# First-rank slots cut from 44 to 22, with a listed tail per graph

## The chip, the cores and the metric

One core of one Trainium2 chip runs the whole program. The metric is device time in microseconds (us) of one execution. A profiled execution has a span, from its first to its last instruction, and a little time around it.

## What is computed

The input is eight graphs of 1,024 nodes with 128 features, and for each graph a 1,024 x 1,024 0/1 adjacency matrix. The layer first takes, for each node, the maximum over the (normalised) features of its first 25 neighbours, and then applies a small mixture-of-experts network to each tile of 128 nodes. Cut to what matters:

```python
scores = jnp.where(A != 0, -arange(N), -inf)
vals, idx = top_k(scores, 25)                 # the 25 lowest-numbered neighbours
agg = where(valid, X[idx], -inf).max(axis=2)  # X = layernorm(x)
agg = where(degree <= 25, maximum(agg, 0), agg)
x = x + relu(concat([X, agg]) @ W + b)        # gnn
h = relu(layernorm(x) @ Wi.T + bi)            # ffn, 2 expert layers, one expert per tile of 128
for l in range(2): h = relu(h @ (mean Ws[l] + Wr[l, e]).T + biases + h)
out = x + h @ Wo.T + bo
```

The chance of an edge falls with the node numbers of both its ends, so the first 128 nodes (the hub tile) have many neighbours, and the other 896 have few: in the inputs used, at most 23.

## The kernel before

The program works on one graph per stage. `positions()` walks ten stages (s = 0 to 9) of NS = 44 positions each. Every engine walks the same list, and its work for position p of stage s is written by tables (`MASK_AT`, `RANK_AT`, `TOP_AT`, `GATHER_AT`, `LAYER_AT` and so on). The order on each engine is thus fixed; engines meet only through semaphores. In stage s three graphs are in work: graph s is prepared (`prepare`), the slots of graph s-1 run (`slot`, `one_hot`, `fold_slot`), and the network of graph s-2 runs (`finish`).

Preparing a graph: ScalarE (ACT) turns adjacency rows into a bf16 mask (line 714), SyncE (SP) issues a DMA that transposes it into `at` (L421), and TensorE (PE) multiplies each 128-row tile of `at` by a triangular matrix (L869). The result `rank[j, i]` says that node j is the r-th neighbour of node i within j's tile of 128 (a value from 201 on says that it is none). ACT copies it out (L641).

A slot serves one pair (tile group g, rank r). A one-hot matrix `onehot = (rank == r)` is made by GpSimd (POOL, L547), by VectorE (DVE, L975), or by ACT in one or two steps (L670 and L687, or L681 for r = 1). PE multiplies the features of the tile by it, once for each of the two parts into which the float32 features are split (L777), which puts the feature row of the r-th neighbour under each node. DVE folds the slot into one of two running maxima (L988). There are two slot banks in PSUM, so PE waits for the fold of the slot before last. A one-hot is 896 columns wide, or less where `CAPS` says that no further tile of nodes needs that rank. One group holds two tiles, 5 and 6. `CAPS` has up to 10 ranks for the first tile and 4 to 6 for the others: 44 pairs.

The hub tile goes another way: DVE finds the 25 neighbours with rounds of max and match-replace (L1039 to L1061), POOL fetches one row per neighbour with 25 indirect DMAs (L535), and DVE reduces them (`reduce_half`). In stage 1 the expert weights are also folded and stored (L908, L1153).

`merge` (L995) joins both maxima after the last slot. `check_totals` (L1177) tests at the end whether any node exceeded its caps; if so, `again` recomputes its tile alone. In the profiled execution no such tile is recomputed.

## Time and profile before

| what | us |
|---|---|
| median of 3 runs | 738.79 (737.64 to 739.55) |
| span of the profiled execution | 734.5 |
| PE busy | 611.5 (83%) |
| DVE busy | 574.2 (78%) |
| POOL busy | 541.9 (74%) |
| ACT busy | 521.2 (71%) |
| DMA, mean rate | 179 GB/s |

The profiled execution's own time is its span of 734.5 us and about 4.3 us around it. Busy time is a union: a pipelined matmul overlaps the next, so the busy time of a group of matmuls contains part of its neighbours' time. The granted clock of PE is given as a share of 2.4 GHz: 0.50 means 1.2 GHz.

### The profile page before, as it was taken

The page shows a single profiled execution, that of the slowest core. Times are in us where ns is not written, and L with a number is a line of the kernel's source. Part 1 is how long each engine was busy: PE and PEld are TensorE (multiplying, and loading weights), DVE is VectorE, ACT ScalarE, POOL GpSimd, SP SyncE. Part 2 cuts the span into 40 slices and gives each one's busy share as a digit, 9 for nine tenths or more (in the row PEclk, how much of TensorE's full clock was granted, in tenths as well). Part 3 has the DMA queues.
Part 4 walks back from the last instruction along what each step waited for, and adds up shares of the span by engine and source line. Part 5 has one row for each costly group of instructions (what it writes and reads, how often), then busy time and mean ns, then how long its engine had stood idle before and what let it go on. Part 6 is the DMA issues. An engine that isn't in the chain of part 4 may idle for free.

```text
span 734.5 us, 11755 instructions
## 1 busy us (share of the span) xinstructions
PE 611.5 (83%) x3496; PEld 502.9 (68%) x3497; DVE 574.2 (78%) x959; ACT 521.2 (71%) x981; POOL 541.9 (74%) x388
## 2 busy tenths in 40 slices
PE   0466666679999799979997999899987999799686
PEld 0054545566987588858885888668875988588565
DVE  3766799878987898779987898789878987777740
ACT  5672455369977898779876987699769985478062
POOL 4577488497979987898878897989799878984000
PEclk9986798898999899979998999989998999799989
DMA  9999997479746965496638755785474543045222
GB/s 298 305 196 265 314 344 241 134 176 293 226 132 158 267 175 152 102 259 205 166 109 222 236 163 142 190 240 159 127 182 124 161 138 87 22 113 144 58 72 77
DMA packets 145171, 131.73 MB, mean 179 GB/s; under 512 B 72219, under 2 KB 112324, under 8 KB 145092
## 3 DMA queue, kind: packets, MB, share of 16 engines
q1 hardware_dynamic: 128124, 105.94, 53.5%
q0 software_dynamic: 7296, 15.74, 8.3%
q10 hardware_dynamic: 9680, 9.21, 4.5%
q8 instruction: 31, 0.51, 0.3%
q14 instruction: 40, 0.33, 0.1%
HBM read 98.20 MB, written 17.98 MB: 158 GB/s over the span
## 4 chain that ended last, share of the span: by engine, by line
PE 59%; DVE 22%; issue 5%; DVEq 4%; DMA 4%; ACT 4%; SPq 1%; ACTq 0%
PE slot_ps L777 28%; PE ffn_ps L842 11%; DVE acc L988 9%; PE ffn_ps L852 4%; PE ffn_ps L826 4%; PE prep_ps L869 3%; DMA at<-mask 2%; PE ffn_ps L811 2%; PE ffn_ps L792 2%; DVEq L1060 2%; DVE top L1047 2%; PE ffn_ps L812 2%; DMA adj_sb<-in_adj_dram 2%; DVE wst L1153 1%; DVE score L1049 1%
## 5 line engine op out<-in xcount | busy, mean ns | idle before, releaser
L777 PE MATMUL slot_ps<-onehot,xsplit 128*128 128x512 f32 (+3 forms) x1376 | 375.5, 401 | 51.1 <-DVE acc L988 44.4
L988 DVE TENSOR_TENSOR acc<-slot_ps,acc 128x896 f32<-128x896 f32 (+2 forms) x336 | 293.7, 884 | 77.3 <-PE slot_ps L777 74.5
L547 POOL TENSOR_SCALAR onehot<-rank,ranks 128x896 fp32r<-128x896 bf16 (+3 forms) x128 | 298.4, 2333 | 72.6 <-PE slot_ps L777 67.5
L777 PEld LDWEIGHTS slot_ps<-onehot,xsplit 128*128 128x128 f32 x1376 | 251.9, 204 | 105.7 <-issue 71.0
L535 POOL DMA_INDIRECT gath<-feature_table,idx x200 | 207.7, 1038 | 47.9 <-issue 42.6
L842 PE MATMUL ffn_ps<-hT,wst 128*128 128x128 f32 x1024 | 135.1, 277 | 0.0
L842 PEld LDWEIGHTS ffn_ps<-hT,wst 128*128 128x128 f32 x1024 | 129.0, 191 | 5.9 <-issue 0.8
L670 ACT ACTIVATE away<-rank,ranks 128x896 bf16<-128x896 bf16 (+4 forms) x136 | 107.9, 793 | 6.8 <-DVE wst L1153 6.4
L687 ACT ACTIVATE onehot<-away 128x896 fp32r<-128x896 bf16 (+4 forms) x136 | 96.3, 708 | 21.5 <-PE slot_ps L777 10.6
L629 ACT ACTIVATE hT<-ffn_ps,wst 128x128 f32<-128x128 f32 x256 | 81.1, 375 | 29.5 <-PE ffn_ps L842 27.3
L641 ACT ACTIVATE rank<-prep_ps 128x448 bf16<-128x448 f32 x128 | 63.0, 550 | 21.0 <-PE prep_ps L869 11.7
L714 ACT ACTIVATE mask<-adj_sb 128x1024 bf16<-128x1024 uint32 x56 | 58.0, 1047 | 25.8 <-DMA at<-mask 20.9
L681 ACT ACTIVATE onehot<-rank,ranks 128x896 fp32r<-128x896 bf16 (+1 forms) x48 | 56.0, 1167 | 22.1 <-PE slot_ps L777 21.3
L869 PE MATMUL prep_ps<-at,before 128*128 128x448 bf16 x128 | 39.9, 380 | 15.0 <-DMA at<-mask 12.3
L908 PE MATMUL ffn_ps<-ident,hT 128*128 128x128 f32 x136 | 26.5, 329 | 28.8 <-DVE wst L1153 25.7
L908 PEld LDWEIGHTS ffn_ps<-ident,hT 128*128 128x128 f32 x136 | 18.8, 169 | 38.8 <-issue 36.7
L1047 DVE MAX8 top<-score 128x8 f32<-128x1024 f32 x32 | 39.0, 1219 | 0.3
L975 DVE TENSOR_SCALAR onehot<-rank,ranks 128x1792 fp32r<-128x1792 bf16 (+2 forms) x40 | 38.5, 962 | 0.7 <-PE slot_ps L777 0.7
L826 PE MATMUL ffn_ps<-xnT,wiT 128*128 128x512 f32 x64 | 33.4, 611 | 0.5 <-ACT xnT L618 0.5
L852 PE MATMUL ffn_ps<-woT,hT 128*128 128x128 f32 x256 | 32.8, 281 | 0.0
L869 PEld LDWEIGHTS prep_ps<-at,before 128*128 128x128 bf16 x128 | 11.4, 99 | 30.9 <-DMA at<-mask 12.4
L852 PEld LDWEIGHTS ffn_ps<-woT,hT 128*128 128x128 f32 x256 | 29.8, 191 | 3.6 <-issue 3.6
(121 smaller groups left out, 586.3 us busy)
## 6 DMA issues: line engine op xcount, KB each, us to landing
wst<-folded_weights SPq DMA_DIRECT2D x128, 257.0 KB, 2.9
adj_sb<-in_adj_dram SPq DMA_DIRECT2D x64, 512.0 KB, 5.9
folded_weights<-wst ACTq DMA_DIRECT2D x34, 256.0 KB, 6.9
hT<-in_L_ffn_Wr_dram SPq DMA_DIRECT2D x26, 256.0 KB, 10.3
xs<-in_x_dram SPq DMA_DIRECT2D x8, 512.0 KB, 8.1
feature_table<-xn SPq DMA_DIRECT2D x8, 512.0 KB, 4.1
x<-in_x_dram SPq DMA_DIRECT2D x8, 512.0 KB, 4.3
out_dram<-h SPq DMA_DIRECT2D x16, 256.0 KB, 2.4
```

Of the source, the lines that this page charges most:

```text
L535: pool.indirect_dma_start(gath[:, j, :], None, tables[b], bass.IndirectOffsetOnAxis(ap=idx[:, b % 2, 0, j:j + 1], axis=0)).then_inc(signal ...
L547: pool.tensor_scalar(onehot[:, UNIT[n]:UNIT[n] + many, 0:wide * P], rank[:, b % 2, first:first + many, 0:wide * P], ranks[:, r - 1:r], Non ...
L629: ins = act.activation(hT[:, 1 - l, j, i, :], ffn_ps[(i + 1) % 2][:, j * P:(j + 1) * P], ACT.Relu, bias=wst[:, i, HC * HID + j:HC * HID + ...
L641: act.activation(rank[:, s % 2, jt, c * CW:(c + 1) * CW], prep_f[c][:, 0:CW], ACT.Copy, bias=float(NONE)).then_inc(s_q, 1)
L670: act.activation(away[:, i % AWAYS, 0:wide * P], rank[:, b % 2, first, 0:wide * P], ACT.Square, bias=ranks[:, r - 1:r], scale=-1.0).then_i ...
L687: act.activation(onehot[:, UNIT[n], 0:wide * P], away[:, i % AWAYS, 0:wide * P], ACT.Relu, bias=1.0, scale=-1.0).then_inc(s_acthot, 1)
L777: mm = pe.matmul(slot_ps[n % 2][:, c0:c1], xsplit[:, b % 2, part, first + j, :], onehot[:, UNIT[n] + j, c0:c1], start=(j == 0 and part == ...
L826: pe.matmul(ffn_ps[1 - j][:, :], wiT[:, j * P:(j + 1) * P], h0T[:, 4 * g:4 * g + 4, :].rearrange("p t c -> p (t c)"), start=True, stop=Tru ...
L842: mm = pe.matmul(ffn_ps[(i + 1) % 2][:, j * P:(j + 1) * P], wst[:, i, c0:c0 + P], hT[:, l, kc, i, :], start=(kc == 0), stop=(kc == HC - 1))
L852: mm = pe.matmul(o, hT[:, 0, kc, i, :], woT[:, kc, :], start=False, stop=(i % 4 == 3 and kc == HC - 1))
L869: mm = pe.matmul(prep_f[c][:, 0:CW], before[:, :], at[:, jt, cols], start=True, stop=not second)
L988: dve.tensor_tensor(acc[:, p % 2, 0:cols], slot_ps[n % 2][:, 0:cols], acc[:, p % 2, 0:cols], ALU.max).then_inc(s_max, 1)
```

## The change

The two-dimensional `CAPS` become one number per source tile, 5, 3, 3, 3, 2, 2, 2, 2, for all 896 nodes: 22 pairs. Every slot is 896 columns wide, and no group holds two tiles. A stage now has NS = 46 positions, and a slot comes at every second one, so a stage has 23 slots: the 22 and a last one for the crowd.

The crowd of a graph is the nodes that have more neighbours in some source tile than the cap. They are listed (at most 128), and what their slots missed (at most 7 neighbours each) is fetched. The steps for graph s-1 in stage s:

- SP stores the last row of `rank` (the counts per tile) at position 37 of stage s-1, as before, and now loads it back at position 40 in pieces of 8 nodes (`counts`).
- DVE compares with the caps and scans (position 1), PE sums over the pieces (2), DVE makes a place for each crowd node (3), PE turns it into a list with 8 small matmuls (4), DVE forms row numbers and columns (5).
- POOL fetches the 128 adjacency rows, 4 KB each, with one indirect DMA (6). ACT makes a mask of them (11), SP transposes it (12), PE ranks it with 8 matmuls of 128 columns (17), DVE keeps the entries beyond the caps and takes the top 8 (18 to 20).
- POOL fetches 7 feature rows for each crowd node, one indirect DMA each (23 to 28). DVE takes their maximum (33), ACT and POOL split it (34, 35), DVE makes a one-hot with which node each list place belongs to, and PE puts them back in slot 22, at position 44.

`x` of the next graph has one buffer instead of two, and is loaded after the feature table is stored. The positions of some other steps move. `check_totals` tests the tail and the length of the list instead. Cut to its core:

```diff
+CAPS = [5, 3, 3, 3, 2, 2, 2, 2]
+TAIL = 7
 PLACES = [
-          (1, 3), (5, 1), (6, 2), (1, 2), (3, 6), (0, 4), ...   # 44
+          (0, 2), (0, 1), (1, 1), (0, 3), (1, 2), (2, 1), (2, 2), (0, 4), (1, 3), (3, 1), (2, 3), (4, 1),
+          (3, 2), (3, 3), (5, 1), (0, 5), (4, 2), (6, 1), (5, 2), (7, 1), (6, 2), (7, 2)]
-NS = len(SLOTS)
+CROWD = len(PLACES)
+NSL = len(PLACES) + 1
+NS = 2 * NSL
-ACT_HOT = [0, 1, 2, 4, 6, 8, 9, 11, 14, 17, 21, 22, 25, 26, 29, 30, 32, 34, 35, 37, 39, 40, 41]
-POOL_HOT = [3, 5, 7, 10, 12, 15, 16, 18, 23, 27, 28, 31, 33, 36, 38, 43]
+POOL_HOT = [0, 4, 8, 12, 16, 20]
+DVE_HOT = [7, 15, CROWD]
+ACT_HOT = [k for k in range(NSL) if k not in POOL_HOT and k not in DVE_HOT]
...
-               {16: 0, 18: 1, 20: 2, 22: 3, 28: 4, 32: 5, 37: 6, 38: 7}]
+               {19: 0, 21: 1, 23: 2, 25: 3, 27: 4, 29: 5, 32: 6, 35: 7}]      # RANK_AT
-              [11, 13, 17, 20, 21, 22, 25, 27]]
+              [11, 13, 15, 17, 21, 23, 25, 27]]                              # TOP_AT
-    REDUCE_AT = {14: (0, 0, 0), 24: (0, 0, 1), 31: (0, 1, 0), 34: (0, 1, 1)}
+    REDUCE_AT = {9: (0, 0, 0), 24: (0, 0, 1), 30: (0, 1, 0), 37: (0, 1, 1)}
+    TAIL_AT = {23: [0], 24: [1, 2], 25: [3], 26: [4], 27: [5], 28: [6]}
...
-        xs = sb("xs", [P, 2, IT, C])
+        xs = sb("xs", [P, IT, C])
...
+                if 1 <= s <= B and p == CROWD_MASK_AT + 1:                   # SP
+                    sp.wait_ge(s_mask, n + 1)
+                    sp.dma_start_transpose(ct[:, :, :], mask[:, n % MASKS, :]).then_inc(s_turn[n % MASKS], 16)
...
+                if s < B and p == COUNT_LOAD_AT:
+                    sp.wait_ge(s_cstore[s % 2], 16 * (s // 2 + 1))
+                    sp.dma_start(counts[0:PIECES, :, :], totals_d[s].rearrange("j (p c) -> p j c", c=EIGHT)
+                                 ).then_inc(s_count, 16)
...
+                if p == FETCH_AT:                                            # POOL
+                    pool.wait_ge(s_fetch, b + 1)
+                    pool.indirect_dma_start(crow[:, :], None, adj_rows,
+                                            bass.IndirectOffsetOnAxis(ap=fetch[:, 0:1], axis=0)
+                                            ).then_inc(s_crow, 16)
+                for i in TAIL_AT.get(p, []):
+                    if i == 0:
+                        pool.wait_ge(s_cidx, b + 1)
+                    pool.indirect_dma_start(tail[:, i, :], None, tables[b],
+                                            bass.IndirectOffsetOnAxis(ap=cidx[:, i:i + 1], axis=0)
+                                            ).then_inc(s_tail, 16)
...
+                if p == CROWD_MASK_AT:                                       # ACT
+                    act.wait_ge(s_crow, 16 * (b + 1))
+                    act.activation(mask[:, n % MASKS, :], crow[:, :].bitcast(U32), ACT.Sign).then_inc(s_mask, 1)
...
+                if p == OFFSET_AT:                                           # PE
+                    pe.wait_ge(s_upto, b + 1)
+                    pe.matmul(prep_f[0][0:PIECES, 0:EIGHT], strict[0:PIECES, 0:PIECES], upto[0:PIECES, :],
+                              start=True, stop=True).then_inc(s_offset, 1)
+                if p == LIST_AT:
+                    pe.wait_ge(s_place, b + 1)
+                    for c in range(EIGHT):
+                        mm = pe.matmul(prep_f[1][:, 0:4], hot[0:PIECES, c, :], ids[0:PIECES, c, :],
+                                       start=(c == 0), stop=(c == EIGHT - 1))
+                if p == BEYOND_AT:
+                    pe.wait_ge(s_turn[n % MASKS], 16 * (n // MASKS + 1))
+                    for jt in range(IT):
+                        mm = pe.matmul(prep_f[half][:, place_ * P:(place_ + 1) * P], ct[:, jt, :],
+                                       beyond[:, STEP_OF[jt], :], start=True, stop=True)
...
-                    second = [f for f, many in GROUPS if many == 2 and f + 1 == jt]
-                        if second:
-                            mm = pe.matmul(prep_f[c][:, 0:CW], onesb[:, :], at[:, jt - 1, cols],
-                                           start=False, stop=True)
...
+                if p == FLAG_AT:                                             # DVE
+                    dve.wait_ge(s_count, 16 * (b + 1))
+                    step(dve.scalar_tensor_tensor(out=kept[0:PIECES], in0=counts[0:PIECES], scalar=NONE - 0.5,
+                                                  in1=unkept[0:PIECES], op0=ALU.is_ge, op1=ALU.mult))
+                    step(dve.tensor_tensor(kept[0:PIECES], kept[0:PIECES], counts[0:PIECES], ALU.add))
+                    step(dve.tensor_tensor(kept[0:PIECES], kept[0:PIECES], limit[0:PIECES], ALU.is_gt))
+                    step(dve.tensor_reduce(flag[0:PIECES, :], kept[0:PIECES].rearrange("p j c -> p c j"), AX_X, ALU.max
+                                           ).then_inc(s_flag, 1))
...
+                if p == TAIL_MAX_AT:
+                    dve.wait_ge(s_tail, 16 * TAIL * (b + 1))
+                    dve.tensor_reduce(tail_max, tail.rearrange("p k c -> p c k"), AX_X, ALU.max).then_inc(s_tailmax, 1)
```

## Rows read from the trace of the kernel before

**Rows 1.** Windows: stages 1, 4, 8 (busy, clock, DMA share, GB/s); below them L995.
```profile
core 0: us, PE busy (x) PEld busy (x) DVE busy (x) ACT busy (x) POOL busy (x), PEclk, DMA share, GB/s
48.00:147.90 99.90, 67.61 (x317) 51.96 (x317) 81.83 (x129) 45.51 (x67) 67.37 (x48) 0.79 0.92 254
303.50:381.10 77.60, 71.88 (x422) 60.46 (x421) 66.09 (x106) 65.12 (x126) 66.34 (x43) 0.93 0.69 181
614.00:688.80 74.80, 68.51 (x405) 58.39 (x404) 55.01 (x84) 43.40 (x89) 50.90 (x32) 0.93 0.33 89
...
L995 DVE TENSOR_TENSOR aggT<-acc x8: 1091/1093/1093, 146.8 to 687.7; 128x896 f32<-128x896 f32 x8
```

**Rows 2.** Windows: positions 0 to 18, 19 to 34, 35 to 43 of stage 4.
```profile
302.30:338.10 35.80, 31.27 (x149) 24.31 (x148) 28.07 (x49) 29.60 (x56) 31.15 (x20) 0.86 0.85 218
338.10:366.60 28.50, 27.83 (x200) 25.95 (x198) 26.06 (x38) 25.52 (x56) 25.70 (x16) 1.00 0.56 155
366.60:380.00 13.40, 12.88 (x78) 10.30 (x76) 12.04 (x22) 10.46 (x15) 9.59 (x7) 1.00 0.53 146
```

**Rows 3.** Groups by line in stage 4: busy us, mean ns, idle before.
```profile
L777 PE MATMUL slot_ps<-onehot,xsplit 128*128 128x512 f32 (+3 forms) x172 | 47.2, 401 | 5.7 <-DVE acc L988 5.6
L547 POOL TENSOR_SCALAR onehot<-rank,ranks 128x896 fp32r<-128x896 bf16 (+3 forms) x17 | 40.2, 2366 | 5.5 <-PE slot_ps L777 5.0
L988 DVE TENSOR_TENSOR acc<-slot_ps,acc 128x896 f32<-128x896 f32 (+6 forms) x42 | 36.8, 884 | 8.6 <-PE slot_ps L777 8.2
L535 POOL DMA_INDIRECT gath<-feature_table,idx x25 | 26.1, 1044 | 5.9 <-issue 5.3 <-DVE idx L1061 0.7
L670 ACT ACTIVATE away<-rank,ranks 128x896 bf16<-128x896 bf16 (+4 forms) x18 | 13.9, 771 | 0.0
L687 ACT ACTIVATE onehot<-away 128x896 fp32r<-128x896 bf16 (+4 forms) x19 | 13.3, 701 | 0.7
L629 ACT ACTIVATE hT<-ffn_ps,wst 128x128 f32<-128x128 f32 x32 | 10.2, 378 | 3.0 <-PE ffn_ps L842 2.7
L641 ACT ACTIVATE rank<-prep_ps 128x448 bf16<-128x448 f32 x16 | 7.9, 553 | 1.1 <-PE prep_ps L872 0.6 <-PE prep_ps L869 0.4
L681 ACT ACTIVATE onehot<-rank,ranks 128x896 fp32r<-128x896 bf16 (+1 forms) x6 | 7.0, 1168 | 1.5 <-PE slot_ps L777 1.5
L1047 DVE MAX8 top<-score 128x8 f32<-128x1024 f32 x4 | 4.9, 1219 | 0.0
L975 DVE TENSOR_SCALAR onehot<-rank,ranks 128x1792 fp32r<-128x1792 bf16 (+2 forms) x5 | 4.5, 905 | 0.0
```

**Rows 4.** The same, shapes kept apart.
```profile
L547 POOL TENSOR_SCALAR onehot<-rank,ranks 128x896 fp32r<-128x896 bf16 x14 | 37.3, 2671 | 5.4 <-PE slot_ps L777 5.0
L988 DVE TENSOR_TENSOR acc<-slot_ps,acc 128x896 f32<-128x896 f32 x28 | 30.1, 1084 | 7.4 <-PE slot_ps L777 7.1
```

**Rows 5.** PE's instructions in order: start us, us, what.
```profile
347.38 1.06 PE L777 MATMUL slot_ps<-onehot,xsplit 128*128 128x512 f32 x4
348.29 1.05 PE L842 MATMUL ffn_ps<-hT,wst 128*128 128x128 f32 x8
```

**Rows 6.** Windows inside positions 5 to 11 of stage 4.
```profile
316.00:321.00 5.00, 2.25 (x6) 1.45 (x6) 4.33 (x18) 1.95 (x4) 4.31 (x5) 0.74 1.22 260
321.00:326.00 5.00, 3.54 (x12) 3.04 (x12) 3.95 (x6) 5.00 (x11) 4.65 (x4) 0.50 0.89 188
```

**Rows 7.** DVE's L1057, 25 elements a row: all eight executions, ns.
```profile
L1057 DVE TENSOR_SCALAR spread<-top,lane x8: 231/2246/2250, 34.1 to 587.7; 128x25 f32<-128x25 f32 x8
```

**Rows 8.** Time to landing of the transposes (`at`), then of adjacency tiles.
```profile
DMA to landing us min/median/max: 3.2/5.6/14.2
...
DMA to landing us min/median/max: 3.5/5.9/9.4
```

**Rows 9.** Windows: stage 1 in two parts, same columns as Rows 1.
```profile
48.00:110.00 62.00, 41.49 (x190) 31.73 (x190) 48.10 (x76) 28.17 (x43) 43.36 (x33) 0.78 1.12 298
110.00:147.90 37.90, 26.12 (x128) 20.23 (x127) 33.72 (x54) 17.34 (x24) 24.01 (x16) 0.82 0.59 182
```

481 lines of the change are left out of this document (312 added, 169 removed), and 5 rows, old and new, of the table PLACES.

## The prediction

> **What bounds the kernel now.** I read the windows by stage first. Stages 2 to 7 are alike: about 77.5 us each (the eight merges of L995 begin at 146.8 to 687.7, seven steps of 77.3 on average [rows 1]), and stage 4 stands for them. In it PE is busy 71.9 of 77.6 us, POOL 66.3, DVE 66.1, ACT 65.1, and DMA has a share of 0.69 [rows 1]. POOL also has 5.3 us of issue gaps between its gathers that count as idle [rows 3], which makes 71.6. So no engine stands alone as the bound: PE is first, POOL is level with it, and the others are 6 us behind. The stage is 1.08 times the busiest engine.
>
> Then the stage in three parts, because its limits differ [rows 2]. In positions 19 to 34 (28.5 us) PE is busy 27.8 at full clock: there PE is the bound. In 35 to 43 (13.4 us) it is so again, 12.9. In positions 0 to 18 (35.8 us) PE shows 31.3, but at a mean clock of 0.86; the norm, the transposes of `h0` and the fold of slots hand over to each other there, and for some 10 us PE runs at half clock (a mean of 0.86 is 28% of the time at 0.50): after a stretch in which it was busy 2.25 of 5 us the granted clock is 0.50, the 1.2 GHz level [rows 6]. PE's idle time before slots, 5.7 us, ends with DVE's fold [rows 3]. DMA is full around these rows, share 0.89 to 1.22 [rows 6]. The three parts add up to 77.7.
>
> **The change on each engine, stage 4.**
>
> PE. The old slots stream 71,168 columns per graph (the sum over `SLOTS` of width x tiles x 2 parts), the new ones 23 x 2 x 896 = 41,216. A slot of 1,792 columns with its four matmuls takes 348.29 - 347.38 = 0.91 us of PE [rows 5], 0.508 ns a column, so 29,952 columns fewer are 15.2 us. The second matmuls of the two-tile group go too (2 x 2 of 448 columns at the same rate, 0.5 us with the pipeline). Added are 17 small matmuls; the trace has none of 4 to 8 columns, so they lie between 0.05 and 0.15 us each (8 matmuls of 128 columns take 1.05 us from first to last [rows 5], 0.13 each, and most of these stream less): 0.9 to 2.6, I take 1.3. PE: 71.9 - 15.2 - 0.5 + 1.3 = 57.5.
>
> DVE. Folds: 36.8 for L988 [rows 3] and 2.2 for the first two (L986, priced as two full folds of 1.084 [rows 4]) become 23 x 1.084 = 24.9, 14.1 less. The one-hots, 4.5 [rows 3], become three of 896 columns, half of the 1,792 form, some 0.6 each: 2.7 less. The crowd adds: five small instructions with drains at position 1, at 0.2 to 0.3 each, 1.3; the place with its compare of 1,024 elements, priced as the MAX8 over 1,024 (1.22 [rows 3]), 1.4; two columns, 0.3; the masking from PSUM in two halves, 1.4; one MAX8, 1.2; two small ones, 0.5; the tail's maximum over 896 elements, priced as a fold, 1.1. Sum 7.2 (below 5 or above 10 would surprise me). DVE: 66.1 - 14.1 - 2.7 + 7.2 = 56.5.
>
> POOL. Of 40.2 for 17 one-hots [rows 3] 6 x 2.67 = 16.0 stay [rows 4]. Gathers go from 25 to 33, eight more at 1.04 plus 0.22 of issue gap (5.3 / 24) [rows 3]: 10.1. The tail's split is a small tensor_tensor, 0.3 to 0.6. POOL with its gaps: 71.6 - 24.2 + 10.1 + 0.6 = 58.1.
>
> ACT. 13.9 + 13.3 + 7.0 = 34.2 for its one-hots [rows 3] become 14 one-hots and 6 squares, each 896 wide, about 1.0 each: 20; mask and split of the tail add 1.3. ACT: 65.1 - 34.2 + 21.3 = 52.2.
>
> DMA. Added per stage: 0.5 MB of crowd rows, one transpose to the seven, 7 gathers of 64 KB, and 112 x 64 counts in pieces of 16 bytes. At 181 GB/s for 0.69 [rows 1] a full share moves 262 GB/s, so the bytes (1.2 MB) are 5 us of DMA; the counts are not priced by any row, 0 to 4 us. From 53.5 us busy to about 60: at a stage of 69 us a share of 0.87. It is no bound on average, but it is in positions 4 to 17.
>
> **The parts, and what is on the path.** Where PE is the bound, its loss counts until another engine takes over.
> - Positions 19 to 34: eight full slots instead of sixteen of mixed width (27,904 columns): 13,568 columns x 0.508 = 6.9 us less, seven rank pairs instead of four 1.1 more: PE 22. ACT then has 16 pairs of relus (10.2 [rows 3]), 7 rank pairs (7.9 / 8 each [rows 3], 6.9), 4 one-hots and 2 squares (6), 23, and each relu waits for PE and PE for the relu before last. POOL has nine gathers and four first gathers, two one-hots and the split, 24. I take 24.5 instead of 28.5: 4.0 saved.
> - Positions 35 to 45: five slots for nine (14,848 columns to 8,960): PE 3.0 less and one rank pair with its second matmuls less, 9.2; DVE about 10, POOL about 12.5 but five slots ahead. I take 11 instead of 13.4: 2.4 saved.
> - Positions 0 to 18: DVE has 28.1 now [rows 2]. Its folds fall from 16.2 (13 of full width and six narrow ones by `SLOTS`) to 10.6, ten of 1.06 with their overlap, and its one-hots by 2.0, but the fourth top step comes in early (1.2) and the crowd's steps are nearly all here (4.4): 26.1. PE's 31.3 are some 26 without the half clock (10 us at half speed), and 12,544 columns (6.4) and two rank pairs (0.7) less, the small matmuls more, 21 at full clock; it waits for DVE at every handover. I keep the 7.7 us that DVE idles now, less 0.8: 33 instead of 35.8, 2.8 saved.
>
> That is 9.2. New waits: the queue of PE stands at `s_upto`, `s_place` and the crowd's transpose, with slots and gnn matmuls behind; ACT stands at `s_crow` with masks and `h0T` copies behind; DVE stands at the tail (33) with folds behind. The fetch is issued at 6 and wanted at 11, some 7 to 9 us later, and adjacency tiles of the same 512 KB land after 5.9 median [rows 8]. The transpose is issued at 12 behind four adjacency loads for the next graph and wanted at 17, 8 us later, against 5.6 median and 14.2 at most [rows 8]. I charge 1.0 us a stage (bounds: 0, all covered, and 11: the fetch late by 2 and the transpose by 6, both at their maxima, and the tail or the counts late by 3). Net 8.2 a stage, 69.5 for 77.7. For six stages: 49.
>
> Stage 8 has no preparation and DMA at 0.33 [rows 1]; PE (68.5) is alone there, and loses 14.4. DVE and POOL are below it; the front part stays a chain, so I take 9 of 74.8. Stage 1 folds the weights: its first 62 us run at a DMA share of 1.12 and are bound by DMA [rows 9], which gets more to do, about 3 us; the remaining 37.9 have DVE busy 33.7 and give 3 back. Net 0. At its start DVE waits for counts that go to memory and back, with nothing before them to hide it: 3 us lost (0 to 6). Stages 0 and 9 have no slots: 0.
>
> Sum: 49 + 9 + 0 - 3 = 55. The profiled execution has a span of 734.5 and 4.3 around it, 738.8, which is the median of the runs: 738.8 - 55 = 684.
>
> **Two rules of the skill against the rows.** The row shows PE at 1.2 GHz right after a thin stretch [rows 6], and the new kernel has 20% less for PE to do. The Trainium skill (TensorE: Matmul & The Clock Gate, What's actually happening) says that the throttled clock is the default and that activity releases it; by that rule, the trace agrees, thinner work can buy slower work, and the price is the third rival below.
>
> L1057 takes 2.25 us for 25 elements in most stages and 0.23 at least [rows 7]. The Trainium skill (SBUF — State Buffer, Who interferes with whom) says that VectorE and GpSimd share one pair of ports that is locked for a whole instruction. By it, L1057's 2 us would often go, since POOL's one-hots fall from 17 to 6, and some of the new small DVE steps would be held as long; the sum would be the same within 2 us a stage.
>
> **Rivals.**
> 1. More than forecast: the engines stay as well coupled as now, 1.08 x 58.1 = 63 a stage. 14.7 x 6 = 88, stage 8 gives 12, stage 1 3, less 3: 100, so 639. For it: PE waits only for DVE now, and every engine gets lighter. Against: positions 0 to 18 are a chain.
> 2. Slower: the crowd's chain is longer than its cover, and PE's queue stands at the crowd's transpose (position 17) until it lands. The chain is fetch, mask, transpose, one behind the other: at the maxima of the landings 9.4 + 1.0 + 14.2 = 24.6 [rows 8], and some 4 for issues between them, for a cover of 11 positions, some 19 us: 10 late. It decides where PE waits more than 9.2 us a stage. At 11, one of them for counts that come late, it is 10 more than I charge, 684 + 7 x 10 = 754. For it: DMA is full just there [rows 6], and 0.5 MB joins it. Against: the median landings, 5.9 + 1.0 + 5.6, leave 6 us over.
> 3. The low clock spreads over the front part: 21 us of PE work at 1.2 GHz is up to 42, of which half the part at most is so now. At 5 us a stage over seven stages: 719.
> 4. The gain in the front part is nothing and ACT or POOL sets the rest: stage 74, 3.7 x 6 + 4 - 3 = 23, so 716.
> 5. It does not do what it says: a list over 128 or a tail over 7 sends tiles into `again`. In the inputs of the reference a graph has 80 to 97 crowd nodes with at most 7 missed neighbours, so no tile goes there; the trace has no price for one.
>
> **How the numbers follow.** Forecast 684 with 0.50, rival 1 0.17, rival 2 0.11, rival 3 0.13, rival 4 0.08, rival 5 0.01. A measurement of this kernel tells 0.3% (2.2 us) from no change. Slower by more: 0.10; within it 0.02 (the lower edge of rival 2 and the upper of rival 3); faster 0.88. The range reaches half way to rival 1 and past rivals 3 and 4: 652 to 722.
>
> **What would show it.** The merges of stages 2 to 7 lie 69 to 70 us apart; L777 has 92 matmuls a stage; PE is busy 56 to 60, DVE 55 to 58, POOL 50 to 53 and 7 of gaps. Positions 0 to 18 take 33. The waits of PE for the crowd's transpose and of ACT for the fetched rows are below 1 us each. The prediction is wrong if these waits come to several us a stage, if PE's clock in the front part falls below 0.7, or if stage 1 grows by more than 5.

## The result and the profile after

The changed kernel takes 772.4 us (median of four runs, 769.95 to 779.13); the kernel before took 738.3 beside it (737.64 to 739.55). The ratio is 1.0483, 95% interval 1.0435 to 1.053: slower by 34 us. The forecast was 684, faster, with a range to 722; it missed by 88. All medians here are over all executions; in experiments 3, 7 and 10 some executions took over 1.5% longer than the fastest of their kernel, and without those the medians are 733.8, 705.4 and 736.2.

The page of the changed kernel: busy time by engine, and the chain that ended last, by engine and by line.
```profile
PE 536.1 (70%) x2978; PEld 426.3 (55%) x2979; DVE 506.9 (66%) x904; ACT 446.6 (58%) x837; POOL 428.0 (56%) x383
...
PE 42%; DVE 17%; issue 11%; DMA 11%; SPq 8%; ACT 7%; another core or an unknown queue 3%; DVEq 2%; ACTq 0%
```
No engine is above 70% of a longer span. Work went, and idle time came. Windows of stages 1, 4 and 8 (same columns as [rows 1]) and the eight merges, L995 before:
```profile
49.40:154.80 105.40, 62.81 (x259) 47.37 (x260) 73.86 (x125) 34.57 (x51) 54.46 (x46) 0.63 0.92 252
326.80:411.80 85.00, 63.11 (x357) 51.12 (x355) 58.33 (x100) 54.80 (x105) 51.73 (x42) 0.86 0.68 178
651.60:722.00 70.40, 56.72 (x341) 46.60 (x340) 45.72 (x77) 35.11 (x71) 34.51 (x29) 0.88 0.42 114
...
L1176 DVE TENSOR_TENSOR aggT<-acc x8: 1091/1348/2556, 153.8 to 720.7; 128x896 f32<-128x896 f32 x8
```
The window of stage 4 is 85.0 us long for 77.6 (it begins 1.2 us before the merge of stage 3 ends; from merge to merge the stage takes 83.5), and every engine is less busy in it than in [rows 1]. The ends of the merges lie 90.0, 83.2, 83.5, 80.6, 81.6 and 78.7 us apart for stages 2 to 7 (466.0 together before, 497.6 now: 31.6 more). Stage 1 ends 6.9 later, stage 8 is 5.5 shorter, the rest 0.8 longer: 34 in all.

Stage 6, the positions 0 to 18, 19 to 34 and 35 to 43 [rows 2]:
```profile
490.60:529.10 38.50, 24.98 (x122) 18.37 (x121) 24.55 (x47) 27.60 (x44) 22.59 (x18) 0.79 0.96 237
529.10:561.50 32.40, 27.23 (x182) 24.53 (x180) 23.48 (x36) 22.87 (x56) 20.20 (x16) 0.94 0.54 146
561.50:572.00 10.50, 9.23 (x56) 7.21 (x56) 10.06 (x16) 4.46 (x6) 8.90 (x9) 1.00 0.57 140
```
Groups by line in stage 6, those that answer to [rows 3]:
```profile
L886 PE MATMUL slot_ps<-onehot,xsplit 128*128 128x384 f32 x89 | 27.3, 433 | 4.9 <-DVE acc L1121 4.0 <-issue 0.9
L592 POOL DMA_INDIRECT gath<-feature_table,idx x25 | 25.2, 1006 | 6.8 <-issue 6.5
L1121 DVE TENSOR_TENSOR acc<-slot_ps,acc 128x896 f32<-128x896 f32 x21 | 22.7, 1089 | 18.1 <-PE slot_ps L886 12.4 <-issue 3.2 <-remote 2.6
L602 POOL TENSOR_SCALAR onehot<-rank,ranks 128x896 fp32r<-128x896 bf16 x7 | 18.4, 2630 | 7.3 <-ACT rank L735 6.2 <-issue 0.7 <-PE slot_ps L886 0.3
L723 ACT ACTIVATE hT<-ffn_ps,wst 128x128 f32<-128x128 f32 x32 | 10.1, 370 | 8.6 <-PE ffn_ps L971 4.6 <-remote 3.5 <-issue 0.3
L642 POOL DMA_INDIRECT xn<-feature_table,cidx x7 | 7.1, 1009 | 2.0 <-issue 2.0
```
The folds fell as worked out; the idle time ahead of them rose from 8.6 to 18.1. Waits of the whole run (us in total, times, longest), the ones that are new:
```profile
PEld prep_ps L907 <- DMA hot<-mask: 35.5, 6, 13.0
PE prep_ps L907 <- DMA hot<-mask: 31.0, 6, 12.6
DVE acc L1121 <- remote: 30.9, 10, 5.8
ACT hT L723 <- remote: 23.9, 8, 4.2
PE prep_ps L894 <- DVE upto L1136: 18.3, 7, 10.3
DVE kept L1130 <- DMA counts<-neighbour_totals: 10.5, 1, 10.5
```
Two stand out. The first is TensorE at the matmuls of the fetched rows (L907), waiting for their transpose. The second has the releaser "remote", which the kernel before has nowhere: VectorE's fold and ScalarE's relu wait for TensorE's increments (the semaphore counts that tell them that a matmul is done) though the trace records its matmuls as run. Here is the place in stage 6: first GpSimd (start us, us), then PE, DVE and ACT.
```profile
536.03 1.01 POOL L642 DMA_INDIRECT xn<-feature_table,cidx  x1 [0.17 <-issue]
...
543.99 0.94 POOL L642 DMA_INDIRECT xn<-feature_table,cidx  x1 [0.30 <-issue]
551.10 2.54 POOL L602 TENSOR_SCALAR onehot<-rank,ranks 128x896 fp32r<-128x896 bf16 x1 [6.17 <-ACT rank L735]
```
```profile
540.93 1.13 PE L886 MATMUL slot_ps<-onehot,xsplit 128*128 128x512 f32 x4
541.92 1.13 PE L971 MATMUL ffn_ps<-hT,wst 128*128 128x128 f32 x8
547.00 2.05 PE L971 MATMUL ffn_ps<-hT,wst 128*128 128x128 f32 x8 [3.94 <-ACT hT L723]
```
```profile
546.35 1.09 DVE L1121 TENSOR_TENSOR acc<-slot_ps,acc 128x896 f32<-128x896 f32 x1 [2.61 <-remote]
```
```profile
546.23 0.63 ACT L723 ACTIVATE hT<-ffn_ps,wst 128x128 f32<-128x128 f32 x2 [3.52 <-remote]
```
The matmuls of one slot and of one relu's layer are recorded from 540.9 to 543.1, but their five increments (layer, both halves of a rank, slot, layer; the times are those of the trace's semaphore events) all arrive between 546.20 and 546.42; the one ahead of them came at 541.13. All this lies behind seven gathers in a row on GpSimd, 536.03 to 544.93. The same gap is in every stage, at 124, 216, 298, 383, 465, 546, 626 and 697.

### The profile page after: what moved, and what is told of

It reads as the page before. It is cut to its first block, busy times and chain, and to the rows that moved or that the text cites. A ratio compares the mean times of both kernels' runs of the same rounds, so it can differ in the third digit from the quotient of the medians.

```text
span 768.2 us, 10291 instructions
## 1 busy us (share of the span) xinstructions
PE 536.1 (70%) x2978; PEld 426.3 (55%) x2979; DVE 506.9 (66%) x904; ACT 446.6 (58%) x837; POOL 428.0 (56%) x383
## 4 chain that ended last, share of the span: by engine, by line
PE 42%; DVE 17%; issue 11%; DMA 11%; SPq 8%; ACT 7%; another core or an unknown queue 3%; DVEq 2%; ACTq 0%
PE ffn_ps L971 16%; PE slot_ps L886 12%; DMA hot<-mask 7%; DVE acc L1121 6%; SPq L469 4%; PE prep_ps L997 3%; PE ffn_ps L955 3%; DMA at<-mask 2%; SPq L431 2%; PE ffn_ps L981 2%; ACT mask L820 2%; PE ffn_ps L940 2%; ACT h L706 1%; PE ffn_ps L941 1%
## 5 line engine op out<-in xcount | busy, mean ns | idle before, releaser
L1121 DVE TENSOR_TENSOR acc<-slot_ps,acc 128x896 f32<-128x896 f32 x168 | 181.5, 1087 | 171.1 <-PE slot_ps L886 124.0
L886 PE MATMUL slot_ps<-onehot,xsplit 128*128 128x512 f32 x704 | 221.6, 444 | 38.5 <-DVE acc L1121 27.4
L592 POOL DMA_INDIRECT gath<-feature_table,idx x200 | 200.1, 1001 | 56.4 <-issue 51.6
L886 PEld LDWEIGHTS slot_ps<-onehot,xsplit 128*128 128x128 f32 x704 | 142.5, 221 | 73.1 <-issue 59.8
L602 POOL TENSOR_SCALAR onehot<-rank,ranks 128x896 fp32r<-128x896 bf16 x48 | 123.7, 2576 | 84.7 <-PE slot_ps L886 51.6
L971 PEld LDWEIGHTS ffn_ps<-hT,wst 128*128 128x128 f32 x1024 | 135.0, 205 | 35.4 <-issue 31.6
L775 ACT ACTIVATE onehot<-rank,ranks 128x896 fp32r<-128x896 bf16 x64 | 66.5, 1040 | 15.9 <-PE slot_ps L886 7.7
L642 POOL DMA_INDIRECT xn<-feature_table,cidx x56 | 55.5, 992 | 16.8 <-issue 15.9
L581 POOL TENSOR_TENSOR xsplit<-xn,xsplit 128x1024 fp32r<-128x1024 f32 x8 | 19.7, 2459 | 80.5 <-ACT xsplit L755 80.4
L997 PE MATMUL prep_ps<-at,before 128*128 128x448 bf16 x128 | 42.8, 413 | 24.4 <-DMA at<-mask 11.5
L765 ACT ACTIVATE away<-rank,ranks 128x896 bf16<-128x896 bf16 x48 | 49.8, 1037 | 1.8 <-DVE wst L1334 1.8
L780 ACT ACTIVATE onehot<-away 128x896 fp32r<-128x896 bf16 x48 | 45.7, 952 | 7.3 <-PE slot_ps L886 6.9
L948 PE MATMUL ffn_ps<-ident,h 128*128 128x128 f32 x64 | 17.9, 435 | 44.8 <-ACT h L706 31.4
L1040 PE MATMUL ffn_ps<-ident,hT 128*128 128x128 f32 x136 | 32.3, 386 | 23.9 <-DVE wst L1334 14.5
L948 PEld LDWEIGHTS ffn_ps<-ident,h 128*128 128x128 f32 x64 | 11.5, 217 | 51.9 <-ACT h L706 36.2
```

The lines of the kernel that those rows point to most:

```text
L592: pool.indirect_dma_start(gath[:, j, :], None, tables[b], bass.IndirectOffsetOnAxis(ap=idx[:, b % 2, 0, j:j + 1], axis=0)).then_inc(signal ...
L602: pool.tensor_scalar(onehot[:, n % UNITS, :], rank[:, b % 2, g, :], ranks[:, r - 1:r], None, ALU.is_equal).then_inc(s_poolhot, 1)
L642: pool.indirect_dma_start(tail[:, i, :], None, tables[b], bass.IndirectOffsetOnAxis(ap=cidx[:, i:i + 1], axis=0)).then_inc(s_tail, 16)
L775: act.activation(onehot[:, n % UNITS, :], rank[:, b % 2, g, :], ACT.Relu, bias=ranks[:, 1:2], scale=-1.0).then_inc(s_acthot, 1)
L886: mm = pe.matmul(slot_ps[n % 2][:, c0:c1], rows, onehot[:, n % UNITS, c0:c1], start=(part == 0), stop=(part == PARTS - 1))
L971: mm = pe.matmul(ffn_ps[(i + 1) % 2][:, j * P:(j + 1) * P], wst[:, i, c0:c0 + P], hT[:, l, kc, i, :], start=(kc == 0), stop=(kc == HC - 1))
```

## The experiments

Each kernel was timed against the kernel before on the same chip, whose medians there were 735.9, 737.3, 735.4, 737.7 and 734.7 us.

**1. The fewer slots alone.** All work for the crowd is left out (list, fetch, ranking, gathers, tail), so the neighbours beyond the caps are missed; slot 22 repeats rank 1 of tile 0.
```
-    MASKED = TT + 1
+    MASKED = TT
-                if k == CROWD: pe.wait_ge(s_tlo, b + 1)
             def crowd(b, p):          # on every engine
+                return
```


> The changed kernel without any of the crowd's work: no counts loaded, no list, no fetched rows, no crowd mask or transpose, no tail; slot 22 repeats the first rank of tile 0, so 23 full slots stay. Left out: what nodes beyond the caps miss. Theory A (the slots were worth little because positions 0 to 18 are a chain of handovers, and the crowd's waits cost the rest): positions 0 to 18 stay near 35 us, 19 to 34 fall to about 26, the end to 10.5, so 71 to 72 a stage and about 695 us in all; the crowd then costs some 75 us of the changed kernel's 772. Rival B (the fewer slots are themselves harmful: PE at low clock, handovers bare): 740 or more. Rival C (all engines coupled as before): 640 to 660.

665.4 us (664.27 to 668.3), ratio 0.9053 [0.9024, 0.9082]. The slots gain 70 us; the crowd's work costs 107. A stage takes 69.1 on average; one of them:
```profile
342.00:410.50 68.50, 56.42 (x338) 46.38 (x338) 51.12 (x83) 53.15 (x102) 42.72 (x33) 0.90 0.77 205
```

**2. One tail gather of seven.** Six are left out, and VectorE waits for the one.
```
-                for i in TAIL_AT.get(p, []):
+                for i in [i for i in TAIL_AT.get(p, []) if i == 0]:
```


> The changed kernel with one of the seven tail gathers per graph, the other six left out; all the rest of the crowd's chain stays. Theory A (in each stage PE's semaphore increments of positions 24 to 26 arrive some 4 to 5 us late, at the end of POOL's run of seven gathers, and the run is the cause): the gap at position 25 goes, 4 to 5 us in eight stages, so 735 to 742 us. Rival B (the gap has another cause at that position, the expert weights or PE's own queue): the gap stays, 765 to 772 us.

725.8 us (721.84 to 727.14), ratio 0.9873 [0.9855, 0.9891]: six gathers cost 46.6 us. Its trace has no fold and no relu that waits for "remote".

**3. The seven gathers paced**, each from the second on waiting for its position's slot, so that at most two stand together.
```
+    TAIL_AT = {23: [0], 24: [1], 25: [2], 26: [3], 27: [4], 28: [5], 29: [6]}
+                    if i > 0:
+                        pool.wait_ge(s_slot, b * NSL + p // 2 + 1)
                     pool.indirect_dma_start(tail[:, i, :], None, tables[b],
```


> The changed kernel with all seven tail gathers, at positions 23 to 29, each from the second on waiting for the slot of its position, so that they come in twos and not in a run. Theory A (the run in a row holds PE's increments back): gap gone or below 1 us, 737 to 745 us. Rival A2 (seven gathers cost PE their time whenever they come): the gap is spread, total 760 to 772. Rival B (another cause): 768 to 775.

734.0 us (729.12 to 740.35), ratio 0.9965 [0.9934, 0.9996]: 38 us back, with every gather still there. The relus' late increments are nearly gone (1.3 us), but the folds still wait, now at the other gathers of the stage:
```profile
DVE acc L1123 <- remote: 19.2, 8, 3.3
```

**4. Seven gathers in a run, added to the kernel before** (stages 2 to 8, into a spare tile, at position 23).
```
+                if 2 <= s <= B and p == 23:
+                    pool.wait_ge(s_slot, (s - 1) * NS + 22)
+                    for j in range(7): pool.indirect_dma_start(extra[:, j, :], None, tables[s - 1], ...)
```


> The kernel before with seven more gathers per graph into a spare tile, in one run at position 23 of stages 2 to 8, started when slot 21 is done; nothing waits for their data. POOL is busy 66 and 5 of gaps in 77.6, so they cost POOL 8.8 us. Theory A: DVE and ACT get PE's increments 3 to 5 us late once a stage, and with POOL's own load the time rises by 30 to 50 us over seven stages, to 770 to 790. Rival B (only POOL's load counts): POOL 75.6 plus its gaps sets 80 a stage, 755 us, and no gap with late increments of PE in the trace.

788.7 us (788.06 to 789.14), ratio 1.0722 [1.0704, 1.074]: 53 us for seven runs. The waits of its trace:
```profile
DVE acc L999 <- remote: 38.6, 8, 5.6
ACT hT L640 <- remote: 26.9, 10, 4.3
```
The late increments come with the run, in the other kernel too. (One of its own gathers follows at once, so eight stand in a row there.)

**5. GpSimd arithmetic of the same length in their place**, in the kernel before.
```
+                    for j, wide in enumerate((7 * P, 7 * P, 7 * P, 2 * P)):
+                        pool.tensor_scalar(extra[:, 0:wide], rank[:, (s - 1) % 2, 0:wide // P, 0:P], ...)
```


> The kernel before with GpSimd kept busy for some 8.5 us at position 23 of stages 2 to 8 by arithmetic of its own (three 128x896 comparisons and one of 128x256 into a spare tile) in place of the seven gathers in one run, which took 365.7 to 374.3 us in one stage and cost 53 us in all (788.7 against 735.9). Theory A, what costs is that seven gathers in a row hold back TensorE's progress (its increments of 368.5 to 372.9 us arrived together): arithmetic of the same length fits into GpSimd's slack (it sat idle some 19 us a stage of the kernel before), so 737 to 752. Theory B, GpSimd is merely late with its one-hots by the length of the run: 780 to 790, as with the gathers.

792.4 us (791.21 to 794.21), ratio 1.0748 [1.0709, 1.0787]. My theory A fell here: arithmetic costs this kernel as much as gathers. There is no "remote" wait; instead (waits):
```profile
PE slot_ps L786 <- POOL onehot L549: 42.1, 9, 5.5
```
GpSimd builds 16 of 44 one-hots there, and TensorE stands when they are late. The 19 idle us a stage in my expectation were an average over all ten stages; in stage 4 GpSimd idles 11.3 [rows 1], 5.3 of them gaps between gathers [rows 3]. With 8.8 more it comes to 80.4 us for a stage of 77.6, so even the sum had no room; the stages measure 85.3 on average, and what is over the sum goes with these waits. So the kernel before could not tell the two causes apart.

**6. The same seven gathers, one at every other position** (23, 25, ... 35), in the kernel before.
```
-                if 2 <= s <= B and p == 23:
+                if 2 <= s <= B and p in range(23, 37, 2):
```


> The kernel before with the same seven added gathers a stage, but one at each of positions 23, 25, 27, ..., 35 in place of all at position 23. Theory A (a run of gathers without arithmetic between them holds TensorE back): the cost mostly goes, 740 to 755. Theory B (the occupied time of GpSimd, or the gathers' transfers): the same seven gathers cost the same, 775 to 790.

765.0 us (761.75 to 766.58), ratio 1.036 [1.0319, 1.04], between both expectations: spreading halves the cost, and 28 us stay, beside 29.1 us in which TensorE waits for GpSimd's one-hots.

**7. The transpose ahead of the loads**, on the paced version.
```
                     if p == TOP_AT[s > 0][0] + 1 and s + 1 < B:     # four adjacency loads
+                    # ahead of them on SP's queue, at p == CROWD_MASK_AT + 1:
+                        sp.dma_start_transpose(ct[:, :, :], mask[:, n % MASKS, :])
```


> The paced version (734.0) with one step moved on SP's queue: the transpose of the fetched rows' mask is issued ahead of the next graph's four adjacency loads at position 12, not behind them. TensorE waited for this transpose 31 to 33 us in all (12.6, 8.2, then 2.3 to 3.0 us in the changed kernel's stages 1 to 6). Theory A, it is late because it stands behind 2 MB of loads: most of the wait goes, 708 to 720. Theory B, it is late because the fetched rows are late (list, fetch and mask make a chain of their own), or the loads now become late instead: 728 to 740. The computation is whole.

707.8 us (703.42 to 715.02), ratio 0.9632 [0.9566, 0.9698]. It beats both kernels. First the queue of SP in the changed kernel, then in this one:
```profile
344.48 7.01 SPq L469 DMA_TRANSPOSE at<-mask  x3
351.53 2.28 SPq L431 DMA_DIRECT2D adj_sb<-in_adj_dram  x4
354.36 3.08 SPq L489 DMA_TRANSPOSE hot<-mask  x1
```
```profile
393.97 1.23 SPq L476 DMA_TRANSPOSE hot<-mask  x1
395.24 2.00 SPq L431 DMA_DIRECT2D adj_sb<-in_adj_dram  x4
```
In the changed kernel TensorE then came to these matmuls and waited until 362.07, 7.7 us after the issue:
```profile
362.07 0.62 PE L907 MATMUL prep_ps<-beyond,hot 128*128 128x128 bf16 x8 [3.01 <-DMA hot<-mask]
```
In the new order the waits fell from 31.0 us (32.7 in the paced version) to 8.2 in two places, and a stage took 73:
```profile
443.70:516.80 73.10, 58.13 (x364) 47.37 (x362) 60.64 (x99) 55.52 (x107) 50.26 (x41) 0.93 0.80 210
```

**8. No wait for the transpose**, on the paced version: TensorE reads a stripe of `at` instead (the ranks beyond the slots mean nothing here), and VectorE gets two waits that keep the order.
```
-                    n = crowd_mask(b)
+                    n = mask_number(min(b + 1, B - 1), 0)
-                       ... ct[:, jt, :], beyond[:, STEP_OF[jt], :]
+                       ... at[:, jt, 0:P], beyond[:, STEP_OF[jt], :]
```


> The paced version (734.0) whose matmuls over the fetched rows read a stripe of the graph's own transposed adjacency, which landed long before, in place of the fetched rows' transpose: TensorE has all its matmuls and no wait there (the ranks beyond the slots are meaningless in this run; the transpose itself is still made). Theory A, TensorE's 31 us in this wait are all on the path: 700 to 708. Theory B, other work that is late anyway takes the place of half of it or more: 718 to 730. The difference to the run with the transpose first says how much of the wait the order on SP's queue explains.

708.4 us (703.66 to 711.64), ratio 0.9585 [0.9529, 0.9642]. That is what the order alone gave: the wait is worth 26 us of the 31 it lasts, and the order explains it.

**9. Arithmetic for the run, in the changed kernel** (the seven rows are not fetched).
```
-                    pool.indirect_dma_start(tail[:, i, :], None, tables[b], ...)
+                    pool.tensor_scalar(tail[:, 0:wide, :], down[:, 0:wide * P]..., ranks[:, 0:1], None, ALU.is_equal)
```


> The changed kernel (772.4) with its seven tail gathers replaced by GpSimd arithmetic of the same length (three 128x896 and one 128x256 operation, some 8.7 us) at the same positions 23, 24 and 25, on the same first waits; the seven rows are not fetched in this run. In the kernel before arithmetic cost as much as the gathers (792.4 against 788.7), so there GpSimd's time alone explained it. Theory A, in the changed kernel too it is GpSimd's time, whatever it does: 765 to 780. Theory B, here it is the run of gathers and its late increments (DVE and ACT waited 31 and 24 us in all for TensorE's increments that came in bursts), not GpSimd's time: 722 to 740, as with one gather (725.8).

726.2 us (724.2 to 732.38), ratio 0.9897 [0.9842, 0.9952]. GpSimd is taken as long as by the run, and 46 us are back. The timeline and all that is left of the folds' "remote" waits:
```profile
504.95 8.88 POOL L646 TENSOR_SCALAR xn<-down,ranks 128x896 f32<-128x896 f16 x4
```
```profile
DVE acc L1124 <- remote: 1.5, 1, 1.5
```
Theory B holds: in the changed kernel GpSimd has time to spare, and it is the run of gathers that costs.

**10. Three and four.** One wait, ahead of the fourth gather.
```
+                    if i == 3:
+                        pool.wait_ge(s_slot, b * NSL + 14)
```


> The changed kernel (772.4) with one wait added in the run of seven gathers: the fourth gather waits for slot 14 (position 26), so that they go as three and four. The computation is whole. Theory A, the length of the unbroken run matters: 732 to 748, near the version with a wait before every gather (734.0). Theory B, each gather costs TensorE its own share or GpSimd's time is what counts, and the full pacing won by moving the gathers late: 752 to 772.

740.0 us (731.12 to 746.14), ratio 1.0019 [0.9972, 1.0065]: at least 32 of the 38 us of full pacing. No fold or relu waits for "remote".

**11. The list later in stage 1**, on the version with the transpose first. The list's steps come four positions later there, and the mask, the transpose and the next graph's loads three.
```
+    LATER = 4
+    def early(b, p): return p - LATER if b == 0 and p - LATER <= FETCH_AT else -1 if b == 0 else p
```


> The version with the transpose first (707.9), and in stage 1 alone the list's steps four positions later (flags at 5 to fetch at 10, mask at 14, transpose and the next loads at 15). In stage 1 VectorE waited 10.2 us for the counts (they landed at 48.3 to 51.4 us) and TensorE 9.8 us behind it at position 2. Theory A, that wait delays everything behind it: 698 to 704. Theory B, stage 1 is bound by its transfers (DMA busy 0.9 and over in its first slices) and takes the time back: 705 to 711. The computation is whole.

717.7 us (713.01 to 718.85), ratio 0.9732 [0.9683, 0.978]: 10 us worse by the medians (the intervals of the two just overlap), outside both expectations. Stage 1 ends at 156.7 for 146.0. VectorE no longer waits for counts, but 20.8 us in one place of stage 1 for an adjacency tile. SP's queue had stood for 12.5 us at a transpose there, and the next adjacency load left at 74.2 us instead of 61.0:
```profile
DVE score L1236 <- DMA adj_sb<-in_adj_dram: 43.8, 7, 20.8
```
TensorE then waits 11.5 us for the crowd's transpose. That alone is not the loss: in experiment 17 it waits 14.7 there, and stage 1 ends at 146.9.

**12. One tail gather, on the version with the transpose first.** The edit of experiment 2.

> The version with the transpose first and paced gathers (707.9) with six of the seven tail gathers left out, as they were from the changed kernel (772.4 to 725.8, 46.6 us). Theory A, paced gathers hide in GpSimd's idle time and hold back nothing: 698 to 708. Theory B, GpSimd's time counts even when paced (48 gathers of 0.97 us and as many gaps of 0.3 us, 61 us in all): 665 to 690. What is left above the version without any of the further rows' work (665.4) is the list, the fetch, the transpose and its ranking.

698.9 us (696.75 to 700.02), ratio 0.9491 [0.9453, 0.9529]: paced, six gathers cost some 9 us in place of 46.6.

**13. The run as plain DMAs** in the changed kernel (the rows are not the listed ones).
```
-                    pool.indirect_dma_start(tail[:, i, :], None, tables[b], ...)
+                    pool.dma_start(tail[:, i, :], tables[b][i * P:(i + 1) * P, :])
```


> The changed kernel (772.4) with its seven tail gathers, in their one run at positions 23 to 28, made plain DMAs from GpSimd's queue: 128 rows of 512 bytes each from the same table into the same tile, without an index (the rows fetched are not those listed). With arithmetic of the same length in their place it took 726.2. Theory A, what holds TensorE's increments back is the transfers of the run (seven times 64 KB in packets of 512 bytes): 760 to 780. Theory B, it is the work of an indexed gather on GpSimd: 720 to 735.

731.4 us (728.13 to 737.29), ratio 0.9922 [0.9899, 0.9945]. The same bytes in the same packets hold almost nothing back (one fold waits 4.3 us for "remote"). But four plain DMAs take GpSimd 2.31 us, 0.6 each and not 1.25 with the gap, so its pace differs too.

**14. The other 25 gathers paced too.**
```
+                            if 2 <= s <= B and p > 0:
+                                pool.wait_ge(s_slot, (s - 1) * NSL + (p + 1) // 2)
                             gather(b, j)
```


> The version with the transpose first and paced tail gathers (707.9), and the other 25 gathers of a stage paced too: each waits until the slot of its position (rounded up, less one) is done in stages 2 to 8. Runs of five gathers are left in that version, and VectorE and ScalarE wait 11.2, 4.6, 4.6 and 2.0 us for increments that came late. Theory A, these runs hold TensorE back as the run of seven did: 690 to 702. Theory B, five in a row cost nothing much and the waits only delay GpSimd: 706 to 722. The computation is whole.

709.7 us (704.52 to 712.18), ratio 0.9625 [0.9595, 0.9655]: nothing gained over 707.8. But the edit did not do what it was meant to. Most of the slots waited for were done already: the trace has 14 runs of five and 8 of six after the first 60 us, for 15 and 8 without the waits, and still 12.7 us of folds and relus at "remote" (15.8 without). So it says nothing on whether runs of five or six cost time.

**15. A plain copy for the transpose**, with the matmuls of experiment 8 (their ranks mean nothing).
```
-  sp.dma_start_transpose(ct[:, :, :], mask[:, n % MASKS, :])
+  sp.dma_start(ct[:, 0, :], mask[:, n % MASKS, 0:P])
```


> The version with the transpose first (707.9), the fetched rows' transpose replaced by a plain copy of an eighth of the mask, and the matmuls of the fetched rows reading a stripe of the graph's own adjacency (their ranks are meaningless in this run). Removing only the wait for the transpose gave 708.4 on the paced version. Theory A, the transpose itself (8 of them, 256 KB each, and some 1.2 to 3 us of SP's queue) delays the loads behind it: 690 to 702. Theory B, it costs nothing once nobody waits for it: 703 to 710.

707.6 us (700.04 to 709.54), ratio 0.9562 [0.9498, 0.9626]: the transpose costs nothing once nobody waits for it.

**16. The list alone**: counts, flags, places and list stay; fetch, mask, transpose, ranking, gathers and tail are left out.
```
-                if p == FETCH_AT:   (and CROWD_MASK_AT, BEYOND_AT, TAIL_HI_AT, TAIL_LO_AT, TAIL_MAX_AT)
+                if False:
```


> The changed kernel without fetch, mask, transpose, ranking and gathers of the further rows, but with the list: counts loaded, flags, running number, TensorE's two small matmuls and VectorE's answers at positions 1 to 5 (slot 22 repeats rank 1 of the first tile). Without any of it 665.4; with all of it but six gathers, and the transpose first, 698.9. Theory A, the handovers between VectorE and TensorE at the front of the stage are what is left (33 us), since both carry the layer's chain there: 682 to 698. Theory B, they are small operations in gaps, and only stage 1's wait for the counts shows: 666 to 678.

670.6 us (668.21 to 675.4), ratio 0.9105 [0.9067, 0.9143]: the list costs some 5 us.

**17 and 18. TensorE's wait for VectorE's scores**: ranking one position later, or the fetched rows' matmuls one earlier.
```
-               {19: 0, 21: 1, 23: 2,
+               {20: 0, 22: 1, 23: 2,
```
```
-    BEYOND_AT = 17
+    BEYOND_AT = 16
```


> The version with the transpose first (707.9) with the first two steps of the next graph's ranking one position later (20 and 22 for 19 and 21). TensorE waited there 1.6 us in each of seven stages, 11.1 in all, until VectorE had scored the further rows in the same banks. Theory A, that wait is on TensorE's path and is part of the 28 us that fetching and ranking the further rows cost (698.9 against 670.6): 697 to 703. Theory B, VectorE carries the path there (its further work is 39 us over the two versions) and the wait only moves: 704 to 712. The computation is whole.

> The version with the transpose first (707.9) with the further rows' matmuls one position earlier (16) and VectorE's three steps on them too (17, 18, 19). The transpose was issued at 394.0 us of one stage, and the matmuls ran at 399.7 without a wait, after those of position 16 from 397.3. Theory A, the transpose has landed by then and the wait of 1.6 us at the ranking is filled by a slot: 697 to 704. Theory B, TensorE now waits for the transpose at position 16 by as much or more: 707 to 720. The computation is whole.

706.6 us (705.27 to 712.74) and 706.8 us (703.72 to 712.23), ratios 0.9636 [0.9583, 0.9688] and 0.9605 [0.9575, 0.9636]. The 11.1 us of this wait are gone from both traces and the time does not change. The crowd's transpose holds TensorE longer in stage 1 of both (14.7 and 9.5 us for 6.2), but that stage ends only 0.9 and 1.5 us later, and stages 2 to 7 take 74.0 and 74.6 on average for 73.7.

**The sum.** From 772.4: pacing the run gives 38.4, the order on SP's queue 26.1, the six gathers even when paced 8.9, fetch, mask, ranking and tail 28.3, the list 5.2, and 665.4 is left: 107 us for the crowd. The kernels ran on several chips, and the intervals of the ratios are 0.3 to 0.7% to each side, so each step is known to some 4 to 6 us.

## Why the prediction was wrong

**The engines' sums: right within 4 us.** PE was forecast at 57.5; it is 58.1 in the version with the transpose first and 61.4 in stage 6 of the changed kernel, part of it at the low clock. In that stage DVE is 58.1 (forecast 56.5), POOL 51.7 and 8.5 of gaps (58.1 with gaps), ACT 54.9 (52.2). One sum in them is wrong: positions 19 to 34 of the kernel before stream 25,856 columns, not 27,904, so 11,520 fewer and 5.9 us for the 6.9. With the slots alone the stage takes 69.1; the forecast was 69.5, but it had the crowd's work in it.

**"I charge 1.0 us a stage": the step that failed.** Stages 2 to 7 took 82.9 on average for 69.5, 80 of the 88 us. Three things were in it. The first two are worth 64.5 us of the 107; with both changed the kernel is at 707.8, still 24 over the forecast.

First, a cost that was in no term: with seven gathers in a row, nothing between them, VectorE and ScalarE wait 2 to 6 us for TensorE's increments once a stage. I priced the eight gathers on POOL's sum (10.1 us) and found POOL below the bound. By that sum they fit: arithmetic of the same length costs nothing there. The kernel before has at most three in a row (once five, in stage 1), so no row of it shows the effect; its price is 46 us for six of the gathers, and a single wait after the third gives at least 32 of it back. Positions 19 to 34 came out at 32.4 for my 24.5, and this gap is why they are longer and not shorter: from TensorE's first ranking matmul for the next graph to the end of the merge it is 43.0 us in the changed kernel (average of stages 2 to 7) and 36.9 with one tail gather (experiment 2).

Second, the transpose. I saw that it is "issued at 12 behind four adjacency loads" and took the median landing of other transposes, 5.6 us, for it. But 2 MB of loads were given out just ahead: in the example it was issued 2.8 us after the first load and landed 7.7 us after its issue. The loads are needed a stage later, the transpose five positions later. The wait was 12.6 and 8.2 us in stages 1 and 2, 2.3 to 3.0 in stages 3 to 6, none in 7 and 8. Its worth is 26 us.

Third, the steps from the fetch to the ranking. They were charged to the engines' sums and, in the front part, only as less idle time ("the 7.7 us that DVE idles now, less 0.8"). The part from the merge's end to the first ranking matmul (position 19) takes, averaged over stages 2 to 7, 32.2 us with the slots alone, 32.3 with the list (experiment 16), 37.5 with fetch, mask, transpose, ranking and one tail gather (12), 36.4 with all seven paced (7), and 40.0 in the changed kernel (one trace each; they scatter by about 1 us). The rest of the stage is 37.0 and 36.4 in experiments 16 and 12. So the 28 us between these two lie in front of position 19 and not in the tail.

**Positions 0 to 18: wrong in sign.** 38.5 for my 33 (35.8 before). With the slots alone this part is near the forecast; the chain got the crowd's own steps, some 5 us, and the transpose's wait, 2.5 us in this stage. The clock is lower too, 0.79 for 0.86: rival 3 saw it, but over a whole stage the version with the transpose first has 0.93, as the kernel before, for 0.87 in stage 6 of the changed one. So the low clock goes with the waits here; no run shows it as a cause of its own. **The end of the stage**: 10.5 for 11, right.

**Stage 8**: 5.5 saved for 9. **Stage 1**: 6.9 lost for 3. The counts held VectorE up 10.5 us for my 3 (bound 6): they go to memory and back through a full queue. The transpose held TensorE 12.6 more; in the new order the stage ends at 146.0, 2 us earlier than before.

**The rivals.** Rival 2, the only slower one (754, 0.11), named the right place and the right queue. It took the fetch, the mask and the transpose at their longest landings; the delay came from the loads ahead and was 2 to 13 us instead of 10. Alone it would not have made the kernel slower: without the run's effect the changed kernel is at 734. Its measure, "more than 9.2 us a stage", was met in stage 1 alone: these waits are 31 us in eight stages. Rival 4 (716: a stage of 74, no gain in the front part) is what the kernel comes to once both are changed, 73.7 a stage and 707.8, but not for its reason: TensorE is busy 24.5 of 25.0 us from 480 to 505 there, so neither ACT nor POOL sets that part. Rival 1 (639) wanted the coupling of before, 1.08 times the busiest engine; even without any crowd a stage is 69.1 over PE's 56.4, 1.22 times, and the time 665. Rival 5 plays no part. The range's lower edge, 652, reaches further than half way to rival 1, which would be some 661.

**The rule on ports.** VectorE's small `spread` operation took 2.25 us in most stages [rows 7]. Now:
```profile
L1238 DVE TENSOR_SCALAR spread<-top,lane x8: 229/231/304, 33.5 to 627.1; 128x25 f32<-128x25 f32 x8
```
The delay of 2 us is gone and was worth little, as the prediction said, but not because the one-hots fell from 128 to 48: six of the eight still run beside one. First the kernel before, then this one:
```profile
351.80 5.05 POOL L547 TENSOR_SCALAR onehot<-rank,ranks 128x896 fp32r<-128x896 bf16 x2
354.64 2.25 DVE L1057 TENSOR_SCALAR spread<-top,lane 128x25 f32<-128x25 f32 x1
```
```profile
551.10 2.54 POOL L602 TENSOR_SCALAR onehot<-rank,ranks 128x896 fp32r<-128x896 bf16 x1 [6.17 <-ACT rank L735]
551.97 0.23 DVE L1238 TENSOR_SCALAR spread<-top,lane 128x25 f32<-128x25 f32 x1
```
The Trainium skill (SBUF — State Buffer, Who interferes with whom) says that where VectorE uses the ports that it shares with GpSimd, the one that issues first holds them for its whole instruction. The trace agrees before, where `spread` begins 0.3 us after the second one-hot and ends with it, and does not now, where it begins 0.87 us after the start and is not held. Over all traces, `spread` and its like for the crowd (`cspread`) are held until some 1.05 us after a one-hot's start when they begin up to 0.7 us after it (unless the one-hot follows another at once, as before), are not held when they begin 0.87 to 1.5 us after it, and `spread` is held to the one-hot's end when it begins 1.7 us after or later. So where the operation falls decides, and the forecast was right here by luck.

**What stays open.** Why a run of indexed gathers makes TensorE's increments late. It is not the time that GpSimd is taken (experiment 9). Not the bytes at the pace of plain DMAs (13), which is another pace. Three and four do not show it (10), seven do every time (and eight in the kernel before, 4). Runs of six (the fetch and five gathers) end without such a wait in stages 2 to 8 of the changed kernel, but single runs of five show one of 3 to 5 us in other traces (1, 7), so length is not all of it. The Trainium skill (Perfetto Trace Analysis, DMA Instruction — SWDGE (GPSIMD)) says that GpSimd's own cores generate the descriptors of such a DMA and that the bar in the profile ends there, not with the data. No run here shows the inside. Open too is which step makes the 28 us in front of position 19: fetching, masking or ranking, not the transpose (15), not TensorE's wait for the scores (17, 18). VectorE's busy time is 39 us larger there (509.7 for 470.4 between experiments 12 and 16) and PE's 14 us, but no run took that away alone.

## What to carry to other kernels

Price a transfer by what its own queue was given just ahead of it, not by the median landing of its kind: a load wanted a stage later belongs behind a transpose wanted in five positions, and that order was worth 26 us here. A sum of busy time says whether an engine has room, not whether a block fits in one piece, nor what it does to its neighbours: nine microseconds of GpSimd arithmetic in one piece, once a stage, cost 55 us in a kernel whose GpSimd had 6 us left and whose TensorE needed its results (the sum, 2.8 us a stage, explains 20 of them), and nothing in one that had them early. An edit that adds waits is an experiment only if the trace shows that they held something back (14). When an addition eats a gain, take each part out on its own before giving the whole up: the change was 34 us slower, and with waits that space the gathers and one moved transpose, 30 us faster (707.8) than the kernel before.
